# Masked graph attention on one core: pairs of query tiles, groups of 1024 keys, an unrolled program

## The chip, the cores and the metric

One NeuronCore of a Trainium2 chip runs the whole kernel. The metric is device time in microseconds (us) of one launch, the median of the timed runs. TensorE multiplies, ACT (ScalarE) evaluates functions, DVE (VectorE) does element-wise work and reductions, GpSimd (POOL) does simple element-wise work, and SyncE (SP) issues the transfers of the DMA engines, in its program's order.

## The reference, cut to what matters

N is 4096 nodes, D is 256 features. `h` is the rectified layer norm of `x`.

```
h   = relu(layernorm(x))
lQ  = masked_x @ Wlq ;  lK = h @ Wlk ;  lV = h @ Wlv + blv
s   = where(adj, lQ @ lK.T / 16, -1e9)                     # 4096 x 4096
gs  = (masked_x @ Wgq) @ (mean(h) @ Wgk).T / 16            # one global score a row
es  = masked_x @ Wes                                       # one own score a row
m   = max(rowmax(s), gs, es)
le, ge, ee = exp(s - m), exp(gs - m), exp(es - m)
den = rowsum(le) + ge + ee
res = le/den @ lV + ge/den * gV + ee/den * (masked_x @ Wev + bev)
out = x + maximum(res, masked_x)
```

## The kernel before

Matrices of the large products are split into a high and a low float16 half, and a product is made of three matmuls: low x high, high x low, high x high. `M = Wlq Wlk^T / 16` is folded first, so that the scores of a tile of 128 query rows are `q = mx M` (float32 matmuls, `project`, L523) times `h` transposed (`hT`). `q` is scaled by row and split on DVE (`q_split`, L732); the transposed halves `qT` come from a DMA transpose.

**Prologue.** Eight blocks g of 512 keys: DVE takes statistics of `x` (`h_stats`, L709) and scales (`h_scales`, L718), ACT applies them (`h_apply`, L432) and casts the high half, GpSimd subtracts for the low half (`h_low`), SP transposes (`transpose_h`, L244). TensorE already makes the scores of tile 0 and the value rows `V = h Wlv`, two V products of 256 keys a block (`v_product`, L592). Each engine has its own written order. A V product is made by TensorE at step g = 3 + b (`V_FIRST`), and moved out by ACT (`v_high`, L440) and DVE (`v_low`, L857) at step g = 5 + b (`V_SPLIT`); each pass of ACT or DVE over g does the layer norm of later blocks too.

**Main part.** One step per tile of 128 rows, 32 tiles, as a loop over pairs of steps. Inside a step there are eight blocks b of 512 keys. For each, TensorE makes the scores of the next tile (`scores`, L546, six matmuls of 512 columns into one of two banks) and the value products of four key chunks (`p_times_v`, L561), half a tile behind (`LAG = 4`). A chunk is a matmul of 512 columns (high half of p times both halves of V) and one of 256 (low half of p times high half of V), summed into `ps_u`. GpSimd turns `adj` into a bias of 0 or a large negative number, 1024 columns at a time (`mask_bias`, L379). DVE adds it to the scores while it moves them to `s32` and takes the block's maximum (`add_mask`, L771). When all eight are there `row_max` (L785) gives the negated row maximum, and ACT begins with the tile: `exp_block` (L452) and `p_high` (L458), 512 columns each; DVE subtracts for the low half (`p_low`, L802); SP transposes 1024 keys at a time (`transpose_p`, L260) into `pT`. `weights` and `combine` on DVE and `add_x` on GpSimd (L391) end a tile; `es_values` (L579) is a float32 product for the own term.

Of the kernel before, what the change touches and what calls it, by code (L numbers as in the profile page):

```python
# [5 lines left out]
P = 128  # L17
# [6 lines left out]
H_SCALE = 2.0 ** 11  # L24
P_SCALE = 2.0 ** 15
Q_TOP = 2.0 ** 14
# [3 lines left out]
W_SCALE = 2.0 ** 14  # L30
V_SCALE = 2.0 ** 10


class Tile:

    def __init__(self, pair, offset):
        self.t = pair * 2 + offset
        self.par = offset % 2  # L40
        self.half = pair + offset // 2


def due(n):

    return not isinstance(n, int) or n > 0


def build(nc, x, adj, mxT, mx, WlqT, WlkT, Wlv, blv, WgqT, WgkT, Wgv, bgv, Wes, Wev, bev, out):
    N, D = x.shape  # L50
    T = N // P
    NB = N // BLOCK
    DC = D // P
    SCALE = float(D) ** -0.5
    MB = 4
    MW = N // MB
    BPM = MW // BLOCK
    BPU = 2
    NU = NB // BPU
    LAG = 4  # L60
    EARLY = 5
    V_FIRST = 3
    V_SPLIT = 5
    HURRIED = 3

    XG = 4

    x_groups = x.rearrange("(g j p) d -> g p j d", p=P, j=CPB)

    with ExitStack() as ctx:  # L70
# [6 lines left out]
        def sem(name):  # L77
# [40 lines left out]
        wq_t = sb("wq_t", [P, DC, D])  # L118
        wk_t = sb("wk_t", [P, DC, D])
        wgq_t = sb("wgq_t", [P, DC, D])  # L120
        wgk_t = sb("wgk_t", [P, DC, D])
        wgv_sb = sb("wgv_sb", [P, DC, D])
        bgv_b = sb("bgv_b", [P, D])
        xbarT = sb("xbarT", [P, DC])
        xbar_bc = sb("xbar_bc", [P, DC, P])
        g_sb = sb("g_sb", [P, DC, D])
        w_sq = sb("w_sq", [P, DC, D])
        w_norm = sb("w_norm", [P, D])
        w_inv = sb("w_inv", [P, D])
        w_hl = sb("w_hl", [P, 2, DC, D], F16)  # L130


        adj8 = sb("adj8", [P, 2, N], U8)
        mxT_q = sb("mxT_q", [P, 2, DC, P])
        mxT_f = sb("mxT_f", [P, 2, DC, P])
        xm = sb("xm", [P, 2, 2, D])
        s32 = sb("s32", [P, 2, N])
        qT = sb("qT", [P, 2, 2 * DC, P], F16)
        q_hl = sb("q_hl", [P, 2, 2, D], F16)
        invc = sb("invc", [P, 2])  # L140
        invc_x = sb("invc_x", [P, 2])
        big = sb("big", [P, 2, 2])
        gs_es = sb("gs_es", [P, 2, 2])
        bmax = sb("bmax", [P, 2, NB])
        negm = sb("negm", [P, 2])
        psums = sb("psums", [P, 2, NB])
        mass = sb("mass", [P, 2, 3])
        rows_done = sb("rows_done", [P, 2, D])
        o_sb = sb("o_sb", [P, 2, D])


        bias = sb("bias", [P, N])
        rmax = sb("rmax", [P, 1])
        rclamp = sb("rclamp", [P, 1])
        rpow = sb("rpow", [P, 1])
        cinv = sb("cinv", [P, 1])
        cq = sb("cq", [P, 1])
        mloc = sb("mloc", [P, 1])
        m1 = sb("m1", [P, 1])
        den = sb("den", [P, 1])  # L160
        rden = sb("rden", [P, 1])
        r_u = sb("r_u", [P, 1])
        w3 = sb("w3", [P, 3])
        u1 = sb("u1", [P, D])
        un = sb("un", [P, D])
        e2 = sb("e2", [P, D])
        ur = sb("ur", [P, D])
        r1 = sb("r1", [P, D])
        r2 = sb("r2", [P, D])
        r3 = sb("r3", [P, D])  # L170

        p_hl = shared2[:, :].bitcast(F16).rearrange("p (u a k) -> p u a k", u=NU, a=2)
        pT = shared[:, :].bitcast(F16).rearrange(
            "p (u a c q) -> p u a c q", u=NU, a=2, q=P)

# [5 lines left out]
        s_wqk, s_wg, s_wgv, s_wlv, s_wev, s_bc = sem("s_wqk"), sem("s_wg"), sem("s_wgv"), sem("s_wlv"), sem("s_wev"), sem("s_bc")  # L181
        s_adj = [sem(f"s_adj{i}") for i in range(2)]
        s_mxq = [sem(f"s_mxq{i}") for i in range(2)]
        s_mxf = [sem(f"s_mxf{i}") for i in range(2)]
        s_xm = [sem(f"s_xm{i}") for i in range(2)]
        s_out = [sem(f"s_out{i}") for i in range(2)]

# [802 lines left out]
```

## Time and profile before

| | |
|---|---|
| median of 3 timed runs | 790.59 us (790.18 to 790.66) |
| span of the profiled execution, first to last instruction | 787.8 us |
| timed median less that span | 2.8 us |
| TensorE busy | 760.5 us, 97% |
| DVE busy | 613.9 us, 78% |
| ACT busy | 386.6 us, 49% |
| GpSimd busy | 222.5 us, 28% |
| mean granted TensorE clock | 0.996 of full speed |
| DMA engines' mean busy share, queue 1 | 74.5% |

The profile gives the span of the one profiled execution; it has no time of its own for the whole launch, so the timed median stands beside it. Busy is not the same as working at full rate: the end of each matmul is modelled, and adjacent ones overlap, so their rate is read from start to start.

### The profile page before, as it was taken

The page shows a single profiled execution, that of the slowest core. Times are in us where ns is not written, and L with a number is a line of the kernel's source. Part 1 is how long each engine was busy: PE and PEld are TensorE (multiplying, and loading weights), DVE is VectorE, ACT ScalarE, POOL GpSimd, SP SyncE. Part 2 cuts the span into 40 slices and gives each one's busy share as a digit, 9 for nine tenths or more (in the row PEclk, how much of TensorE's full clock was granted, in tenths as well). Part 3 has the DMA queues.
Part 4 walks back from the last instruction along what each step waited for, and adds up shares of the span by engine and source line. Part 5 has one row for each costly group of instructions (what it writes and reads, how often), then busy time and mean ns, then how long its engine had stood idle before and what let it go on. Part 6 is the DMA issues. An engine that isn't in the chain of part 4 may idle for free.

```text
span 787.8 us, 15535 instructions
## 1 busy us (share of the span) xinstructions
PE 760.5 (97%) x4200; PEld 424.8 (54%) x4200; DVE 613.9 (78%) x1811; ACT 386.6 (49%) x871; POOL 222.5 (28%) x175
## 2 busy tenths in 40 slices
PE   4799999999999999999999999999999999999995
PEld 3476555555555555555555555555555555555553
DVE  5967677788777778887777788877777888777775
ACT  5757553345555444455554434555544445555442
POOL 2642222332222323322223233223232332132200
PEclk9999999999999999999999999999999999999999
DMA  9983787967778778767677786766777876778656
GB/s 268 227 155 83 145 156 145 174 140 146 144 149 160 148 152 169 147 143 148 141 164 146 154 166 140 156 137 146 162 146 158 167 148 143 143 143 168 119 119 125
DMA packets 334786, 119.92 MB, mean 152 GB/s; under 512 B 303920, under 2 KB 330672, under 8 KB 334768
## 3 DMA queue, kind: packets, MB, share of 16 engines
q1 hardware_dynamic: 334768, 119.70, 74.5%
q8 instruction: 8, 0.13, 0.1%
q14 instruction: 10, 0.08, 0.0%
HBM read 39.98 MB, written 4.19 MB: 56 GB/s over the span
## 4 chain that ended last, share of the span: by engine, by line
PE 82%; issue 7%; DVE 5%; DMA 4%; SPq 1%; ACT 1%; POOL 0%; DVEq 0%; POOLq 0%
PE ps_scores L555 37%; PE ps_u L573 24%; PE ps_u L575 12%; PE ps_q L531 3%; PE ps_v L589 3%; DMA shared<-shared 3%; PE ps_v L602 3%; DMA shared<-x 1%; DVE st L713 1%; DVE shared L805 1%; DVE s L780 1%; DVE w_sq L888 0%; ACT shared L437 0%; DVE q_hl L752 0%; SPq L266 0%
## 5 line engine op out<-in xcount | busy, mean ns | idle before, releaser
L555 PE MATMUL ps_scores<-hT,qT 128*128 128x512 f16 x1536 | 374.3, 380 | 4.9 <-DVE bmax L780 3.5
L573 PE MATMUL ps_u<-v_rows,shared 128*128 128x512 f16 x1024 | 346.2, 379 | 5.8 <-DMA shared<-shared 5.8
L387 POOL TENSOR_SCALAR bias<-adj,big 128x1024 f32<-128x1024 uint8 x128 | 169.8, 1327 | 495.9 <-DVE bmax L780 270.4
L575 PE MATMUL ps_u<-v_rows,shared 128*128 128x256 f16 x1024 | 279.1, 273 | 0.0
L780 DVE CUSTOM_DVE_ANT_0 s<-ps_scores,bias 128x512 f32<-128x512 f32 x256 | 176.3, 689 | 98.4 <-PE ps_scores L555 82.6
L555 PEld LDWEIGHTS ps_scores<-hT,qT 128*128 128x128 f16 x1536 | 149.8, 98 | 160.2 <-issue 6.5
L805 DVE SCALAR_TENSOR_TENSOR shared<-s,shared 128x512 f16<-128x512 f32 x256 | 192.0, 760 | 20.1 <-ACT shared L464 20.1
L454 ACT ACTIVATE s<-s,negm,invc_x 128x512 f32<-128x512 f32 x256 | 204.5, 799 | 0.0
L506 ACT ACTIVATE mass<-gs_es,negm 128x2 f32<-128x2 f32 x32 | 9.5, 296 | 362.0 <-DVE negm L799 362.0
L573 PEld LDWEIGHTS ps_u<-v_rows,shared 128*128 128x128 f16 x1024 | 100.1, 98 | 131.4 <-DMA shared<-shared 9.7
L464 ACT ACTIVATE shared<-s 128x512 f16<-128x512 f32 x256 | 154.1, 614 | 0.0
L575 PEld LDWEIGHTS ps_u<-v_rows,shared 128*128 128x128 f16 x1024 | 100.2, 98 | 35.5
L396 POOL TENSOR_TENSOR o_sb<-rows_done,xm 128x256 f32<-128x256 f32 x32 | 36.0, 1126 | 42.5 <-DVE rows_done L855 42.5
L454 ACT ACTIVATION_READ_ACCUMULATOR s<-s,negm,invc_x 128x1 f32 x256 | 47.8, 187 | 0.0
L531 PE MATMUL ps_q<-mge,mxT_q 128*128 128x258 f32 (+1 forms) x128 | 34.3, 391 | 1.2 <-issue 1.2
L589 PE MATMUL ps_v<-wev_sb,mxT_f 128*128 128x256 f32 x128 | 32.9, 380 | 0.0
L531 PEld LDWEIGHTS ps_q<-mge,mxT_q 128*128 128x128 f32 x128 | 22.5, 195 | 7.3 <-issue 1.9
L589 PEld LDWEIGHTS ps_v<-wev_sb,mxT_f 128*128 128x128 f32 x128 | 21.8, 190 | 5.4
L376 POOL TENSOR_TENSOR v_rows<-shared,v_rows 128x1024 f16<-128x1024 f32 x8 | 17.2, 2149 | 24.1 <-ACT v_rows L450 24.1
L602 PE MATMUL ps_v<-w_hl,hT 128*128 128x256 f16 x192 | 22.7, 276 | 0.4 <-DVE v_rows L860 0.4
L602 PEld LDWEIGHTS ps_v<-w_hl,hT 128*128 128x128 f16 x192 | 18.9, 100 | 4.8 <-DVE v_rows L860 1.3
L780 DVE DVE_READ_ACCUMULATOR2_ANT bmax<- 128x1 f32 x256 | 21.3, 83 | 0.0
(75 smaller groups left out, 371.4 us busy)
## 6 DMA issues: line engine op xcount, KB each, us to landing
adj<-adj SPq DMA_DIRECT2D x32, 512.0 KB, 4.3
shared<-x SPq DMA_DIRECT2D x8, 512.0 KB, 6.1
mxT_q<-mxT SPq DMA_DIRECT2D x32, 128.0 KB, 2.6
mxT_f<-mxT SPq DMA_DIRECT2D x32, 128.0 KB, 2.2
xm<-x SPq DMA_DIRECT2D x32, 128.0 KB, 2.8
xm<-mx SPq DMA_DIRECT2D x32, 128.0 KB, 2.3
out<-o_sb SPq DMA_DIRECT2D x32, 128.0 KB, 2.3
shared<-shared SPq DMA_TRANSPOSE x128, 4.3
```

Of the source, the lines that this page charges most:

```text
L387: nc.gpsimd.tensor_scalar(bias[:, b * MW:(b + 1) * MW], adj8[:, k.par, b * MW:(b + 1) * MW], big[:, k.par, 0:1], big[:, k.par, 1:2], ALU.m ...
L396: nc.gpsimd.tensor_tensor(o_sb[:, k.par], rows_done[:, k.par], xm[:, k.par, 0], ALU.add).then_inc(s_o, 1)
L454: nc.scalar.activation(s32[:, k.par, b * BLOCK:(b + 1) * BLOCK], s32[:, k.par, b * BLOCK:(b + 1) * BLOCK], ACT.Exp, bias=negm[:, k.par:k.p ...
L464: nc.scalar.activation(p_hl[:, u, 0, at:at + BLOCK], s32[:, k.par, b * BLOCK:(b + 1) * BLOCK], ACT.Copy, scale=P_SCALE).then_inc(s_phi, 1)
L531: last = nc.tensor.matmul(ps_q[:, 0:cols], mxT_q[:, k.par, c], mge[:, c, 0:cols], start=c == 0, stop=c == DC - 1)
L555: last = nc.tensor.matmul(ps_scores[:, b % 2], qT[:, k.par, q_half * DC + c], hT[:, b * CPB:(b + 1) * CPB, h_half * DC + c, :], start=firs ...
L573: nc.tensor.matmul(ps_u[:, k.par], pT[:, u, 0, at + j], v_rows[:, kc, :], start=kc == 0, stop=False)
L575: last = nc.tensor.matmul(ps_u[:, k.par, 0:D], pT[:, u, 1, at + j], v_rows[:, kc, 0:D], start=False, stop=kc == NB * CPB - 1)
L589: last = nc.tensor.matmul(ps_e, mxT_f[:, k.par, c], wev_sb[:, c], start=c == 0, stop=c == DC - 1)
L602: last = nc.tensor.matmul(ps_v[:, n % 2, j * D:(j + 1) * D], hT[:, 2 * n + j, h_half * DC + c], w_hl[:, w_half, c], start=first, stop=h_ha ...
L780: nc.vector.tensor_tensor_reduce(out=s32[:, k.par, b * BLOCK:(b + 1) * BLOCK], in0=ps_scores[:, b % 2], in1=bias[:, b * BLOCK:(b + 1) * BL ...
L805: nc.vector.scalar_tensor_tensor(p_hl[:, u, 1, at:at + BLOCK], s32[:, k.par, b * BLOCK:(b + 1) * BLOCK], P_SCALE, p_hl[:, u, 0, at:at + BL ...
```

## The change

The kernel works on pairs of tiles and groups of 1024 keys: 16 pairs times 4 groups are 64 periods p, and one unit u is one tile of a period. The whole program is unrolled.

- **Scores.** Four blocks a period (`classic`): two tiles times two halves of 512 keys, each in its own bank (`ps_w`, `ps_x[1]`, `ps_v`, `ps_x[0]`). Each block is two `product` calls of three matmuls, one for each half of the 256 features, so eight products a period.
- **Values.** A chunk is three matmuls of 256 columns: high x high, high x low, low x high, into one 256-column sum for each tile. They run six periods behind the scores (`LAG_V = 6`), exponentials five (`LAG_E = 5`).
- **ACT.** `mask_bias` is now an ACT Identity with scale and bias by row, 1024 columns from uint8. Exponentials are 1024 wide and carry the factor of p in their bias, and `p_high` is a plain 1024-wide copy. ACT also scales and casts `q` (`q_scale`, `q_high`), in order among the exponentials.
- **DVE.** `out11`, `out12`, `out21`, `out22` take the place of `add_mask`; `p_low` is one 1024-wide subtraction; the scales of a pair's rows are found together (`q_rows`).
- **GpSimd** gets `q_low` and the bias terms of the row's end (`rest`, `add_rest`, `finish`).
- **Buffers.** `s32` holds five periods, `bias` three units, `p_hl` two, `pT` three; the row values of two tiles share a bank.
- **Prologue.** The scores of periods 0 to 3 (two tiles) are made there. `V_AT` gives the step at which V products are made and moved out, the same for TensorE, ACT and DVE.

The core of the diff:

```diff
+        V_AT = {3: (0,), 4: (1, 2), 5: (3, 4), 6: (5, 6), 7: (7, 8), 8: (9, 10, 11), 9: (12, 13, 14, 15)}
+            def transpose_p(u):
+                sp.wait_ge(s_plo, u + 1)
+                if u >= NPT:
+                    sp.wait_ge(s_pv, u - NPT + 1)
...
+            for p in range(4, NPER + LAG_V + 1):
+                if p + 1 < NPER and p >= 4:
+                    load_adj(p + 1)
+                if 0 <= p - LAG_E < NPER:
+                    transpose_p(2 * (p - LAG_E))
...
+                if 0 <= p - LAG_E < NPER:
+                    transpose_p(2 * (p - LAG_E) + 1)
...
+            def mask_bias(u):
+                p, t = u // 2, u % 2
...
+                if u >= NBI:
+                    v = u - NBI
+                    if v % 2 == 0:
+                        act.wait_ge(s_o11, v // 2 + 1)
+                        act.wait_ge(s_o12, v // 2 + 1)
...
+                nc.scalar.activation(bias[:, u % NBI].rearrange("p b k -> p (b k)"), adj8[:, p % 2, t], ACT.Identity,
+                                     bias=big[:, n % 2, 1, t:t + 1], scale=big[:, n % 2, 0, t:t + 1]
+                                     ).then_inc(s_bias, 1)
...
             for g in range(NB):
-                if HURRIED < g < NB - 1:
-                    h_deviation(g + 1)
                 h_apply(g)
-                if g <= HURRIED:
+                if g + 1 < NB:
                     h_deviation(g + 1)
                 h_high(g)
...
+                if g in (2, 4, 6):
+                    mask_bias(g - 2)
+                    mask_bias(g - 1)
+                for n in V_AT.get(g, ()):
                     v_high(n)
...
+            for p in range(4, NPER + LAG_V + 1):
+                if p < NPER:
+                    mask_bias(2 * p + 1)
+                u = 2 * (p - LAG_E)
+                live = 0 <= u < 2 * NPER
+                if live:
+                    if u % (2 * NG) == 0:
+                        act.wait_ge(s_negm, p // NG)
+                    exp_unit(u)
+                    if u % (2 * NG) == 0:
+                        side_exp((p - LAG_E) // NG)
+                    p_high(u)
+                n = (p + 3) // NG
+                if p % NG == 1 and 2 <= n < NP:
+                    q_scale(n)
+                if live:
+                    exp_unit(u + 1)
...
+                if p + 1 < NPER:
+                    mask_bias(2 * p + 2)
+                if live:
+                    p_high(u + 1)
...
+                if p >= 1:
+                    pe.wait_ge(free, p)
...
+                    nc.tensor.matmul(acc, pT[:, u % NPT, 0, j], v_rows[:, kc, 0:D], start=kc == 0 and t == 0,
+                                     stop=False, skip_group_check=True)
+                    nc.tensor.matmul(acc, pT[:, u % NPT, 0, j], v_rows[:, kc, D:2 * D], start=False, stop=False,
+                                     skip_group_check=True)
+                    done = nc.tensor.matmul(acc, pT[:, u % NPT, 1, j], v_rows[:, kc, 0:D], start=False, stop=end,
+                                            skip_group_check=True)
...
+                if b >= 1:
+                    for t in range(2):
+                        classic((b - 1) // 2, t, (b - 1) % 2)
+                for n in V_AT.get(b, ()):
+                    v_product(n)
...
                 if g >= 3:
-                    add_mask(Tile(0, 0), g - 3)
-                if g >= V_SPLIT:
-                    for n in v_steps(g - V_SPLIT):
-                        v_low(n)
-            for b in range(NB - V_SPLIT, EARLY):
-                for n in v_steps(b):
+                    p, b = (g - 3) // 2, (g - 3) % 2
+                    if b == 0:
+                        out11(p)
+                        out21(p)
+                    else:
+                        out12(p)
+                        out22(p)
+                for n in V_AT.get(g, ()):
                     v_low(n)
...
+                if low:
+                    p_low(u)
+                if p < NPER:
+                    out11(p)
+                m = (p + 3) // NG
+                if p % NG == 1 and 2 <= m < NP:
+                    q_rows(m)
+                if low:
+                    p_low(u + 1)
+                if p < NPER:
+                    out21(p)
...
+                if p < NPER:
+                    out12(p)
+                    out22(p)
```

## Rows read from the trace of the kernel before

**Rows 1.** The page: busy time of engines, share of the span, instructions.

```profile
PE 760.5 (97%) x4200; PEld 424.8 (54%) x4200; DVE 613.9 (78%) x1811; ACT 386.6 (49%) x871; POOL 222.5 (28%) x175
```

**Rows 2.** Timeline of TensorE in the middle: start us, us, engine, line, instruction.

```profile
403.64 1.04 PE L531 MATMUL ps_q<-mge,mxT_q 128*128 128x258 f32 x4
404.51 1.46 PE L555 MATMUL ps_scores<-hT,qT 128*128 128x512 f16 x6
405.81 0.38 PE L573 MATMUL ps_u<-v_rows,shared 128*128 128x512 f16 x1
...
407.11 1.46 PE L555 MATMUL ps_scores<-hT,qT 128*128 128x512 f16 x6
```

**Rows 3.** Groups by line: busy us, mean ns, idle us before, releasers.

```profile
L555 PE MATMUL ps_scores<-hT,qT 128*128 128x512 f16 x1536 | 374.3, 380 | 4.9 <-DVE bmax L780 3.5 <-DMA qT<-q_hl 1.5
L573 PE MATMUL ps_u<-v_rows,shared 128*128 128x512 f16 x1024 | 346.2, 379 | 5.8 <-DMA shared<-shared 5.8
...
L805 DVE SCALAR_TENSOR_TENSOR shared<-s,shared 128x512 f16<-128x512 f32 x256 | 192.0, 760 | 20.1 <-ACT shared L464 20.1
...
L387 POOL TENSOR_SCALAR bias<-adj,big 128x1024 f32<-128x1024 uint8 x128 | 169.8, 1327 | 495.9 <-DVE bmax L780 270.4 <-DVE big L756 225.5
```

**Rows 4.** Timeline of TensorE, prologue; idle time before in brackets.

```profile
23.23 1.46 PE L555 MATMUL ps_scores<-hT,qT 128*128 128x512 f16 x6 [1.48 <-DMA qT<-q_hl]
...
31.24 2.72 PE L555 MATMUL ps_scores<-hT,qT 128*128 128x512 f16 x6 [3.45 <-DVE bmax L780]
...
37.33 1.47 PE L555 MATMUL ps_scores<-hT,qT 128*128 128x512 f16 x6
38.66 2.79 PE L602 MATMUL ps_v<-w_hl,hT 128*128 128x256 f16 x24
41.29 0.54 PE L618 MATMUL ps_u<-ones,v_rows 128*128 128x1 f16 x16
```

**Rows 5.** Timelines of TensorE and GpSimd, the end of the span.

```profile
770.46 0.38 PE L573 MATMUL ps_u<-v_rows,shared 128*128 128x512 f16 x1 [3.35 <-DMA shared<-shared]
...
782.00 0.27 PE L575 MATMUL ps_u<-v_rows,shared 128*128 128x256 f16 x1
...
784.76 0.72 POOL L396 TENSOR_TENSOR o_sb<-rows_done,xm 128x256 f32<-128x256 f32 x1 [8.57 <-DVE rows_done L855]
```

**Rows 6.** Timeline of ACT in the middle.

```profile
402.68 0.80 ACT L454 ACTIVATE s<-s,negm,invc_x 128x512 f32<-128x512 f32 x1
...
403.47 0.61 ACT L464 ACTIVATE shared<-s 128x512 f16<-128x512 f32 x1
```

**Rows 7.** Timeline of ACT, prologue.

```profile
30.15 2.06 ACT L437 ACTIVATE shared<-shared,nb_h,rs_h 128x256 f32<-128x256 f32 x4
32.24 1.06 ACT L450 ACTIVATE v_rows<-shared 128x1024 f16<-128x1024 f32 x1
33.22 0.30 ACT L428 ACTIVATE sd<-mv,eps_sb 128x4 f32<-128x4 f32 x1
```

**Rows 8.** Timeline of DVE, prologue.

```profile
15.86 0.42 DVE L736 TENSOR_REDUCE rmax<-ps_q 128x1 f32<-128x256 f32 x1
...
17.07 0.48 DVE L752 TENSOR_SCALAR q_hl<-ps_q,cq 128x256 f16<-128x256 f32 x1
...
31.01 0.17 DVE L722 RECIPROCAL rs<-sd 128x4 f32<-128x4 f32 x1
...
33.10 0.69 DVE L780 CUSTOM_DVE_ANT_0 s<-ps_scores,bias 128x512 f32<-128x512 f32 x1
```

**Rows 9.** The transposes of line 266, from issue to landing.

```profile
DMA to landing us min/median/max: 4.2/4.3/7.1
```

**Rows 10.** Windows of the prologue: busy us by engine, granted clock.

```profile
core 0: us, PE busy (x) PEld busy (x) DVE busy (x) ACT busy (x) POOL busy (x), PEclk, DMA share, GB/s
...
31.30:34.60 3.30, 3.30 (x10) 1.37 (x11) 3.23 (x14) 3.27 (x7) 1.22 (x1) 0.50 1.12 262
34.80:38.00 3.20, 3.20 (x41) 2.59 (x39) 3.17 (x13) 3.17 (x7) 3.20 (x3) 1.00 1.01 192
```

More of the change, by code:

```diff
@@ L130, in build @@
[L130 to L144, printed above, removed]
@@ L161, in build @@
[L161 to L174, printed above, removed]
+        rmax = sb("rmax", [P, 2])
@@ L209, in build @@
+        s_ru, s_f, s_top = sem("s_ru"), sem("s_f"), sem("s_top")
         block = ctx.enter_context(nc.Block())
[L211 to L225 removed]
@@ new lines, in side_exp, with p_high @@
+            def side_exp(n):
+                for t in range(2):
+                    nc.scalar.activation(mass[:, n % 2, t, 1:3], gs_es[:, n % 4, t], ACT.Exp,
+                                         bias=negm[:, n % 2, t:t + 1]).then_inc(s_ge, 1)
+            def p_high(u):
+                p, t = u // 2, u % 2
+                act.wait_ge(s_exp, u + 1)
+                if u >= 2:
+                    act.wait_ge(s_pT[(u - 2) % NPT], ring(u - 2, NPT))
+                nc.scalar.activation(p_hl[:, u % 2, 0], s32[:, p % NS, t], ACT.Copy).then_inc(s_phi, 1)
@@ new lines, in side_scores, with q_form @@
+            def side_scores():
+                pe.wait_ge(s_gev, 3)
+                pe.wait_ge(s_wgv, 32)
+                for n, src in ((0, mxT_q), (1, mxT_f)):
+                    for t in range(2):
+                        for c in range(DC):
+                            last = nc.tensor.matmul(ps_side[:, n, t], src[:, t, c], mge[:, c, D:D + 2], start=c == 0,
+                                                    stop=c == DC - 1)
+                last.then_inc(s_side, 1)
+            def q_form(n, f, hl):
+                return qT[:, n % 2, hl * 4 + f]
@@ new lines, in es_values @@
+            def es_values(n):
+                pe.wait_ge(s_mxf, 16 * (n + 1))
+                if n == 0:
+                    pe.wait_ge(s_wev, 16)
+                if n + 3 < NP:
+                    pe.wait_ge(s_qf, 2 * (n + 4))
+                if n >= 1:
+                    pe.wait_ge(s_c2, 2 * n)
+                for t in range(2):
+                    for c in range(DC):
+                        last = nc.tensor.matmul(ps_q[:, t, 0:D], mxT_f[:, t, c], wev_sb[:, c], start=c == 0,
+                                                stop=c == DC - 1)
@@ L601, in v_product @@
                         for c in range(DC):
[L602 removed]
+                            last = nc.tensor.matmul(bank[:, j * D:(j + 1) * D], hT[:, 2 * n + j, h_half * DC + c],
                                                     w_hl[:, w_half, c], start=first,
@@ L701, in step_ @@
-            def step_(*a, project=True, **k):
-                step(*a, project_=project, **k)
-            schedule(pe, step_)
+            for t in range(2):
+                classic(3, t, 1)
+            for n in V_AT[NB]:
+                v_product(n)
+            side_scores()
+            pe.wait_ge(s_gev, 4)
+            for c in range(DC):
+                last = nc.tensor.matmul(ps_gv, xbar_bc[:, c], wgv_sb[:, c], start=c == 0, stop=c == DC - 1)
+            last.then_inc(s_gstep, 1)
+            for p in range(4, NPER + LAG_V + 1):
+                v = p - LAG_V
+                weigh = 0 <= v < NPER
+                n = (p + 3) // NG
+                if p % NG == 2 and 0 <= (p - 10) // NG < NP:
+                    es_values((p - 10) // NG)
+                if p % NG == 1 and 2 <= n < NP:
+                    project(n, D + 2)
+                at = 0
+                for b in range(2):
+                    for t in range(2):
+                        if p < NPER:
+                            classic(p, t, b)
+                        if weigh:
+                            p_times_v(v, at, at + 4)
+                            at += 4
+                for k in V_AT.get(NB + p - 3, ()):
+                    v_product(k)
```

1008 lines of the change are left out of this document (484 added, 524 removed).

## The prediction

> **What bounds the kernel now.** I read the page's engine row first, then the spacing of TensorE's instructions, then the first 80 us and the last 20, engine by engine. TensorE is busy 97% of the span [rows 1]. That figure hides nothing: in the middle, six 512-column products start 1.30 us before the next group (0.216 us each), four value chunks of a 512- and a 256-column product take another 1.30 us (0.325 a chunk), and the four float32 matmuls of one tile's projection 0.87 us, with no gap between [rows 2]. The `es_values` group has the same form; I price it alike. A tile then costs 8 x 1.30 + 8 x 1.30 + 2 x 0.87 = 22.5 us. All idle time ahead of value products is 5.8 us, and ahead of score products 4.9 us, over the whole span [rows 3]. So the steady part can't be shortened by better overlap. What there is to win or lose lies in the matmuls' own cost, in the start and in the end. From 31.24 us TensorE is dense [rows 4]; before that it starts its first score at 23.23 and idles 3.45 us. At the end it stalls 3.4 us at 770.46 and finishes at about 782.3; the last 5.5 us of the span are the row tail and the store [rows 5].
>
> **TensorE's work.** The score products stay 1536 of 512 columns: "eight" is four blocks of one period times two halves, each three matmuls, which is what there was. Per value chunk the columns stay 768, but as 3 x 256. A 24-matmul V product (all 256 columns, each with its own weights) takes 41.29 - 38.66 = 2.63 us, 0.1096 a matmul [rows 4], so a chunk costs 0.329 instead of 0.325: 1024 x 0.004 = +4 us. (From below nothing, from above 0.0096 x 1024 = +10 if the rounding of rows goes against me.) A period, four score blocks and 16 chunks, is 4 x 1.30 + 16 x 0.329 = 10.46 us; a pair of tiles 4 x 10.46 + 4 x 0.87 = 45.3.
>
> **The other engines in steady state.** An ACT exponential of 512 starts 0.79 us before the next instruction [rows 6]; a 1024-column copy takes 1.06 us, 0.95 of it before the next [rows 7]. For 1024 I take 1.28 (exp) and 0.95 (copy). The mask bias on ACT is not in the trace. Bounds: a 1024-column copy, 0.95, and four 256-column Relus with bias and scale from memory, 2.06 [rows 7]; I take 1.12, near the copy, since it is one instruction. ACT has six such per period: 6.7 us of 10.46. DVE: the mask add 0.61 and accumulator read, four times; the 1024-wide subtraction, from 0.76 at 512 [rows 3], between 1.0 and 1.5, I take 1.25. That is 5 us. GpSimd loses 128 mask instructions of 1.33 us [rows 3] and gets the row tail. What counts is the chain, since each engine runs in program order: ACT's mask bias for the second tile waits for `out12` of the period before; then mask, exp, copy, exp, mask, copy (6.7), then DVE's second `p_low` (1.25), `out21`, `out12` (1.3) and hops (0.2): 9.4 us per period. In one period in four `q_scale` waits on ACT for `cq`, behind the first `p_low`, `out11` and 1.5 us of row scales: with its own work +5.2 us. Four periods 4 x 9.4 + 5.2 = 42.8, under the 45.3 of TensorE. The queue on SP gives a second chain: `p_low`, issue of its transpose (about 2), the adj load behind it (4.3), mask 1.1, copy 1.0, `p_low` 1.25 = 9.7. Both fit, narrowly; each bank is free a whole period before TensorE wants it. I cost the steady part at TensorE's work.
> A section of the Trainium skill, ScalarE: Activation LUTs, "Rules for kernel authors", says multiplications and adds belong on VectorE, not ScalarE. By it, the move of the mask to ACT is the wrong way. The rows give ACT 3.8 us spare a period, so the sum has nothing for it; if it were wrong, it would be rival 1.
>
> **The prologue** is where the change loses. In the old one the copies of V product n run on ACT two key blocks after TensorE makes it, and TensorE cycles in 6.1 and then 4 to 5 us a block [rows 4]. In the new one product n, its `v_high` on ACT and its `v_low` on DVE all stand in the same step g (`V_AT`). Step g+1 on ACT (four Relus, then sqrt) waits behind `v_high`; DVE's `h_scales` waits for that sqrt, and the mask adds of key block g-2 come after it; TensorE's scores need these to free the bank; its V products come after the scores. That is a ring without slack.
> First scores: the first projection starts 13.28 as before, eight matmuls at 0.43 instead of four: 16.9. Reduction of 512 and scales: the old one takes 17.07 - 15.86 = 1.21 with a 256-wide reduction [rows 8], so 1.5: 18.6. ACT scales and copies (new) 1.4: 20.0; GpSimd subtraction of 512 1.1: 21.1; transpose 4.3 [rows 9]: 25.5. Two tiles' block 0: 28.2; block 1, 31.2; mean and second projection, 33.4. DVE's scales 1.5, then `w_hl` low and the first mask add: 36.7. Scores 2.6, V product 2.63, `v_high` 0.8: 42.8.
> The ring: Relus 2.1 [rows 7], sqrt 0.3, `h_scales` 0.5 and `h_stats` 1.6 (31.01 to 33.10) [rows 8], mask add 0.7, hops 0.4, two score blocks 2.6, two V products 5.25, `v_high` 0.6 = 14.0 us. Steps 4 and 5 pay it: 70.8. Step 6 has no `h_stats`: 12.4, 83.2. Step 7 has no scales: 9.9, 93.1. After the loop DVE has four mask adds and the mean, TensorE the g step, two score blocks and three V products before the next eviction: 15.8, 108.9. Side scores and the global value: 112.8. Period 4 with four V products: 5.2 + 10.5 = 128.5, eviction 1.5: 130. Second-pair projection and period 5's scores: 136.9. The first exponential waits on ACT for `v_high` of the last product, so the first value product can't start before 130.6 + 1.1 + 1.3 + 0.4 + 1.0 + 1.25 + 4.3 = 140; unit 1 waits for `q_scale`. I count 5.8 us for this filling: periods 6 and 7 end at 136.9 + 20.9 + 5.8 = 163.6.
> The clock: after the old kernel's 3.45 us of idleness the granted clock stood at 0.50 from 31.3 to 34.6 (1.2 GHz) and then 1.00 (2.4 GHz) [rows 10], and six products took 2.7 instead of 1.46 [rows 4]. That costs 1.7 us of work. The new prologue idles 3.4, 5.6, 5.8, 4.3 and 3.9 us (the steps less TensorE's part). I take four drops: +7, 170.6. Bounds: none, five. The Trainium skill, TensorE: Matmul & The Clock Gate, "HAM oscillation — how this bites in real kernels", describes this pattern of bursts and waits, each burst beginning at the low level; the one idle stretch of the trace agrees.
>
> **The rest.** From there: 56 periods of scores x 5.2 = 291; 62 periods of values x 5.26 = 326; 13 projections of a pair x 1.74 = 23; 16 x 1.74 = 28 for `es_values`: 668, which gives 838.6. Tail: the new lag is six periods, two after the last row maximum is known behind the old half tile. Eight units of pair 15 pass through two p_hl buffers: transpose 4.3 [rows 9], copy 1.05, subtraction 1.25, hops: 6.8 us for two units where TensorE needs 5.3. The first lands 13.5 after the last score, the last at 37.3; plus 2.6 and 1.7: 41.7 against 35.0 of work, +6.7. The last `es_values` stands behind the last value product, then two DVE adds 1.0, GpSimd add of 512 (0.72 at 256 [rows 5], so 1.2), max 0.7, GpSimd 1.2, store 2.6, hops: 7.3 instead of 5.5.
> Sum: 838.6 + 6.7 + 7.3 = 852.6 of span. The old span is 787.8 and its timed median 790.59: 2.8 lie around it. **Predicted 855 us**, 8% slower.
>
> **Rivals.** (1) The steady loop doesn't keep up. For it: chains of 9.4 and 9.7 us against 10.46, and transposes land in up to 7.1 us [rows 9]. If landing takes 1.5 us more and contention 0.4 on each subtraction, the chain passes TensorE's mean of 11.3 by 0.6: 56 x 0.6 = +34, 889 us. Against: TensorE waited for nothing in the old steady part. (2) The ring is looser: part of Relu, stats and V work overlaps, so that each step costs 9 instead of 14, no clock drop: 855 - 4 x 5 - 7 - 5 = 823. For it: the old prologue ran such steps in 4.4 to 6.1. Against: the program order as read. (3) Not slower: the ring doesn't exist because TensorE's queue always holds enough ready work, so that it is dense from its first score at 25.5. Remaining work then is 256 x 1.30 + 337 + 21 + 6 + 26 + 28 = 751; 776.5 + 6.7 + 7.3 = 790.5 of span, and 784 if the tail also doesn't stall: 787 to 793 timed. It decides only if the prologue's idle time after the first score is under about 2 us. I see no mechanism by which TensorE's own work shrinks: that the shared weights of two of three value matmuls load once gains nothing while loads lie under 256 columns [rows 4].
>
> **Numbers.** The unit for "same" is 0.2% (1.6 us), about what a measurement of this kernel can tell. The forecast 0.64 (its own range 838 to 872: no to five clock drops, filling 0 to 12, matmuls 0 to +10); rival 1 0.17; rival 2 0.11; rival 3 0.06, whose 787 to 793 lies astride the old time and is split evenly between faster and same; else 0.02, slower. Low 820 takes in rival 2, high 889 rival 1's centre; outside stay rival 3 and the far half of rival 1. Slower 0.94, same 0.03, faster 0.03.
>
> **What would show it.** Right: step 4's last V product is evicted near 57 us, first value product near 140 to 147, TensorE idle 3 to 6 us before the first score of steps 4 to 6, released by DVE's mask adds, which wait for the sqrt; the clock at 0.5 behind each; a pair of 45.3 us in the middle, without gaps. Wrong: idle time at `ps_x` or `ps_w` or before value products in every fourth period in the middle (rival 1); the first value product before 110 us (2), before 90 (3).

## The result and the profile after

The changed kernel takes **858.27 us** (median of 4 executions, 856.7 to 861.7), the kernel before 790.38 in the same session: ratio 1.087, 95% interval [1.0845, 1.0900]. Slower by 8.7%, 3.3 us above the forecast of 855. The profiled execution has a span of 854.9 us; before it was 787.8.

The page of the kernel after, engine row and granted clock in 40 slices of 21.4 us:

```profile
PE 784.0 (92%) x5232; PEld 535.0 (63%) x5232; DVE 451.0 (53%) x1155; ACT 506.4 (59%) x663; POOL 251.1 (29%) x223
...
PEclk9978799999999999999999999999999999999988
```

TensorE's share fell from 97% [rows 1] to 92%, and no other engine is near full: DVE went down from 78% to 53%. TensorE is still the bound in the long middle (9.9 us are lost there in 540); what the change adds lies in its waits before and after. I put TensorE's spacing at the full rate (0.216 us per 512-column product, 0.109 per 256-column one, 1.74 per pair's projection) against the time that it took, stretch by stretch of the trace. What is left is lost, idle or at half rate (an estimate, good to 3 us a row and to 1 us in the differences between the kernels):

| | before | after |
|---|---|---|
| TensorE's work at full rate | 746.8 | 749.4 |
| lost, first product to 25 us | 10.1 | 13.1 |
| lost 25 to 160 | 11.5 | 54.6 |
| lost 160 to 700 | 0.7 | 9.9 |
| lost 700 to TensorE's end | 4.7 | 14.7 |
| after TensorE's last product, and before its first | 14.0 | 13.3 |
| span | 787.8 | 854.9 |

Of the 67 us, 3 are lost before 25 us and 43 in the rest of the prologue, 9 in the long middle, 10 at the end; 2.6 are in the matmuls themselves.

TensorE's timeline of the kernel after, the scores of steps 4 to 7, the first value product, and the middle (start us, us, line, [idle us before <- releaser]):

```profile
46.46 0.58 PE L564 MATMUL ps_v<-hT,qT 128*128 128x512 f16 x1 [5.33 <-DVE bmax L793]
...
58.85 0.59 PE L564 MATMUL ps_w<-hT,qT 128*128 128x512 f16 x1 [5.34 <-DVE bmax L793]
...
70.35 0.58 PE L564 MATMUL ps_v<-hT,qT 128*128 128x512 f16 x1 [3.82 <-DVE bmax L793]
...
79.14 0.38 PE L564 MATMUL ps_w<-hT,qT 128*128 128x512 f16 x1 [1.73 <-DVE bmax L793]
...
132.93 0.28 PE L604 MATMUL ps_u<-v_rows,pT_base 128*128 128x256 f16 x1 [1.92 <-DMA pT_base<-p_base]
...
422.86 0.28 PE L604 MATMUL ps_u<-v_rows,pT_base 128*128 128x256 f16 x1 [0.86 <-DMA pT_base<-p_base]
```

Before, key blocks came every 4 to 6 us [rows 4]; now steps are 12.4, 11.5 and 8.8 us apart, and ahead of each step TensorE sits idle until DVE's mask adds free a bank (a step has two score blocks now and had one before). What DVE waited for is seen in one turn of the ring, all engines from 50.3 to 58.9 us:

```profile
50.35 1.47 PE L642 MATMUL ps_q<-r_base,hT 128*128 128x256 f16 x12
51.66 1.47 PE L642 MATMUL ps_u<-r_base,hT 128*128 128x256 f16 x12
...
53.17 0.60 ACT L400 ACTIVATE v_rows<-ps_u 128x512 f16<-128x512 f32 x1 [0.71 <-PE ps_u L642]
53.67 2.06 ACT L391 ACTIVATE p_base<-s,nb_h,rs_h 128x256 f32<-128x256 f32 x4
...
55.63 0.28 ACT L383 ACTIVATE sd<-mv,eps_sb 128x4 f32<-128x4 f32 x1
...
55.95 0.18 DVE L742 RECIPROCAL rs<-sd 128x4 f32<-128x4 f32 x1 [1.45 <-ACT sd L383]
...
56.45 1.40 DVE L734 BATCH_NORM_STATS2 st<-s 128x6 f32<-128x256 f32 x4
...
58.04 0.66 DVE L793 CUSTOM_DVE_ANT_0 s<-ps_w,bias 128x512 f32<-128x512 f32 x1
...
58.85 0.59 PE L564 MATMUL ps_w<-hT,qT 128*128 128x512 f16 x1 [5.34 <-DVE bmax L793]
```

Read it as one chain: TensorE's V product (L642), ACT's copy of it (L400), ACT's four normalisations and the sqrt behind that copy (L391, L383), DVE's scales and statistics, the mask add (L793), and only then TensorE's next scores, whose V products close the ring. In a turn TensorE has 5.2 us of work at full rate (twelve score products and two V products); step 4 took 12.39.

Windows of the same prologue, step 4, step 5, step 6, and step 7 to the first value product; the column after POOL is the granted clock:

```profile
46.46:58.85 12.39, 7.05 (x52) 4.29 (x53) 4.68 (x18) 6.00 (x10) 3.23 (x3) 0.78 0.32 64
58.85:70.35 11.50, 7.68 (x52) 4.48 (x53) 3.17 (x10) 4.76 (x9) 0.61 (x2) 0.80 0.82 120
70.35:79.14 8.79, 7.06 (x52) 4.29 (x53) 2.60 (x7) 4.47 (x8) 1.74 (x1) 0.85 0.46 98
79.14:132.90 53.76, 43.82 (x238) 26.86 (x238) 18.51 (x57) 19.91 (x28) 2.12 (x1) 0.84 0.17 40
```

A mean of 0.78 over 12.39 us with levels of 0.5 and 1.0 is 2 x 0.22 x 12.39 = 5.5 us at 1.2 GHz. The four rows give 5.5 + 4.6 + 2.6 + 17.2 = 30 us at the low level, against 3.4 in the whole old prologue [rows 10].

Groups by line of the kernel after (busy us, mean ns | idle us before, releasers), the answers to [rows 3]:

```profile
L604 PE MATMUL ps_u<-v_rows,pT_base 128*128 128x256 f16 x1024 | 281.1, 275 | 20.6 <-DMA pT_base<-p_base 20.5
L831 DVE TENSOR_TENSOR p_base<-s,p_base 128x1024 f16<-128x1024 f32 x128 | 164.8, 1288 | 223.3 <-ACT p_base L461 223.3
...
L434 ACT ACTIVATE bias<-adj,big 128x1024 f32<-128x1024 uint8 x128 | 158.2, 1238 | 189.8 <-DVE bmax L793 166.2 <-DMA adj<-adj 23.4
L447 ACT ACTIVATE s<-s,negm,invc 128x1024 f32<-128x1024 f32 x128 | 157.2, 1228 | 0.0
L461 ACT ACTIVATE p_base<-s 128x1024 f16<-128x1024 f32 x128 | 134.3, 1049 | 21.4 <-DMA pT_base<-p_base 19.7
```

The value products now wait 20.5 us in all for transposes (before 5.8). ACT's three big operations, among them the new mask bias at 1.24 us, fill 450 of its 506 us, and it still has 40% of the span free. In the tail DVE and ACT wait in turn (their timelines):

```profile
825.03 0.69 DVE L866 TENSOR_TENSOR t_sb<-t_sb,xm 128x512 f32<-128x512 f32 x1 [4.87 <-POOL t_sb L352]
...
831.36 1.06 ACT L461 ACTIVATE p_base<-s 128x1024 f16<-128x1024 f32 x1 [4.32 <-DMA pT_base<-p_base]
...
832.45 1.23 DVE L831 TENSOR_TENSOR p_base<-s,p_base 128x1024 f16<-128x1024 f32 x1 [3.38 <-ACT p_base L461]
```

DVE stands 4.87 us in the row work of the tile pair that is done, and a subtraction of the next unit stands behind it; ACT's copy waits for one of the two buffers until its transpose has landed.

### The profile page after: what moved, and what is told of

It is laid out like the page before. It is cut to its first block and busy times, and to the rows that moved or that the text cites. A ratio compares the mean times of both kernels' runs of the same rounds, so it can differ in the third digit from the quotient of the medians.

```text
span 854.9 us, 13952 instructions
## 1 busy us (share of the span) xinstructions
PE 784.0 (92%) x5232; PEld 535.0 (63%) x5232; DVE 451.0 (53%) x1155; ACT 506.4 (59%) x663; POOL 251.1 (29%) x223
## 5 line engine op out<-in xcount | busy, mean ns | idle before, releaser
L604 PE MATMUL ps_u<-v_rows,pT_base 128*128 128x256 f16 x1024 | 281.1, 275 | 20.6 <-DMA pT_base<-p_base 20.5
L831 DVE TENSOR_TENSOR p_base<-s,p_base 128x1024 f16<-128x1024 f32 x128 | 164.8, 1288 | 223.3 <-ACT p_base L461 223.3
L606 PE MATMUL ps_u<-v_rows,pT_base 128*128 128x256 f16 x1024 | 280.7, 274 | 0.0
L608 PE MATMUL ps_u<-v_rows,pT_base 128*128 128x256 f16 x1024 | 280.6, 274 | 0.0
L434 ACT ACTIVATE bias<-adj,big 128x1024 f32<-128x1024 uint8 x128 | 158.2, 1238 | 189.8 <-DVE bmax L793 166.2
L447 ACT ACTIVATE s<-s,negm,invc 128x1024 f32<-128x1024 f32 x128 | 157.2, 1228 | 0.0
L461 ACT ACTIVATE p_base<-s 128x1024 f16<-128x1024 f32 x128 | 134.3, 1049 | 21.4 <-DMA pT_base<-p_base 19.7
L604 PEld LDWEIGHTS ps_u<-v_rows,pT_base 128*128 128x128 f16 x1024 | 100.7, 98 | 65.2 <-DMA pT_base<-p_base 30.5
L606 PEld LDWEIGHTS ps_u<-v_rows,pT_base 128*128 128x128 f16 x1024 | 100.8, 98 | 34.8 <-issue 0.3
L608 PEld LDWEIGHTS ps_u<-v_rows,pT_base 128*128 128x128 f16 x1024 | 100.8, 98 | 12.3
L564 PE MATMUL ps_x<-hT,qT 128*128 128x512 f16 x256 | 99.0, 387 | 3.4 <-DVE bmax L793 3.4
L565 PE MATMUL ps_x<-hT,qT 128*128 128x512 f16 x256 | 98.8, 386 | 0.0
L566 PE MATMUL ps_x<-hT,qT 128*128 128x512 f16 x256 | 98.4, 384 | 0.0
L793 DVE CUSTOM_DVE_ANT_0 s<-ps_x,bias 128x512 f32<-128x512 f32 x128 | 88.2, 689 | 14.0 <-DVE p_base L831 10.2
L564 PE MATMUL ps_w<-hT,qT 128*128 128x512 f16 x128 | 49.7, 388 | 10.9 <-DVE bmax L793 10.9
L564 PE MATMUL ps_v<-hT,qT 128*128 128x512 f16 x128 | 49.9, 390 | 9.2 <-DVE bmax L793 9.2
L793 DVE CUSTOM_DVE_ANT_0 s<-ps_w,bias 128x512 f32<-128x512 f32 x64 | 44.2, 691 | 11.2 <-DVE p_base L831 10.2
L566 PE MATMUL ps_v<-hT,qT 128*128 128x512 f16 x128 | 50.0, 391 | 0.0
L565 PE MATMUL ps_v<-hT,qT 128*128 128x512 f16 x128 | 50.0, 391 | 0.0
L566 PE MATMUL ps_w<-hT,qT 128*128 128x512 f16 x128 | 49.8, 389 | 0.0
```

The lines of the kernel that those rows point to most:

```text
L434: nc.scalar.activation(bias[:, u % NBI].rearrange("p b k -> p (b k)"), adj8[:, p % 2, t], ACT.Identity, bias=big[:, n % 2, 1, t:t + 1], sc ...
L447: nc.scalar.activation(s32[:, p % NS, t], s32[:, p % NS, t], ACT.Exp, bias=negm[:, n % 2, t:t + 1], scale=invc[:, n % 4, t:t + 1], accum_o ...
L461: nc.scalar.activation(p_hl[:, u % 2, 0], s32[:, p % NS, t], ACT.Copy).then_inc(s_phi, 1)
L564: nc.tensor.matmul(bank, q_form(n, f, 1), keys(0), start=start, stop=False, skip_group_check=True)
L565: nc.tensor.matmul(bank, q_form(n, f, 0), keys(1), start=False, stop=False, skip_group_check=True)
L566: return nc.tensor.matmul(bank, q_form(n, f, 0), keys(0), start=False, stop=stop, skip_group_check=True)
```

## Experiments

In each, the kernel before ran on the same chip (789.5 to 789.7 us median). All are edits of the changed kernel except e5 and e6, which edit the kernel before; e11 and e12 add to e10, which joins four of the edits.

**e1: V products moved out one step later.** TensorE makes them where it did; ACT and DVE take most of them a step later, so that the sqrt and the mask adds don't stand behind them.

```diff
+V_OUT = {4: (0,), 5: (1, 2), 6: (3, 4), 7: (5, 6), 8: (7, 8, 9, 10, 11), 9: (12, 13, 14, 15)}
 (ACT's v_high and DVE's v_low:)
-for n in V_AT.get(g, ()):
+for n in V_OUT.get(g, ()):
...
-for n in V_AT[NB]:
+for n in V_OUT[NB]:
```

> The changed kernel, with each V product moved out (v_high on ACT, v_low on DVE) one step after TensorE makes it, instead of in the same step. Theory (ring in the prologue): steps 4 to 7 start their scores every 6 to 7 us instead of every 9 to 12.4, most of the half-rate stretches of the clock go too, the first value product moves from 132.9 to about 105 to 112 us, and the time falls from 858 to 830 (824 to 838). Rival (the steps are long for another reason, such as ACT's own work or landing transposes): another wait takes over, the steps keep 10 us or more, 850 or above.

Measured 832.15 us, ratio 1.053 [1.0500, 1.0568]: 26 of the 68 us, from the order of a few copies. Its V products of steps 4, 5 and 6 and the first score of step 7 (TensorE's timeline):

```profile
46.46 1.47 PE L644 MATMUL ps_q<-r_base,hT 128*128 128x256 f16 x12
...
52.07 1.47 PE L644 MATMUL ps_q<-r_base,hT 128*128 128x256 f16 x12
...
57.68 1.47 PE L644 MATMUL ps_q<-r_base,hT 128*128 128x256 f16 x12
...
63.85 0.39 PE L566 MATMUL ps_w<-hT,qT 128*128 128x512 f16 x1 [3.01 <-DMA hT<-v_rows]
```

Steps of 5.6 us instead of 12.4 and 11.5, with no idle time between; the first value product comes at 110.9 instead of 132.9. From 25 to 160 us the trace has 17 us at the low level where the kernel after has 34; that goes with the ring's idle stretches and is part of the gain. So for these 26 us the ring is the cause, and not the amount of work on any engine, which is the same. From step 6 on the steps are 8.8 and 8.6 us long again: ahead of step 7's scores TensorE waits 3.0 us for a transpose of `h`.

**e2: TensorE kept busy in the ring's idle stretches.** Added matmuls that nothing reads, ahead of the scores of steps 4 to 7.

```diff
+keep_busy({4: 70, 5: 70, 6: 50, 7: 20}.get(b, 0))   # 128-column matmuls into an unread part of ps_u
 if b >= 1:
     for t in range(2):
         classic((b - 1) // 2, t, (b - 1) % 2)
```

> The changed kernel with 70, 70, 50 and 20 added 128-column matmuls, whose sums are used by nothing, ahead of the scores of steps 4 to 7, where TensorE idles. The ring is left as it is; only the clock should change. Theory (half-rate stretches behind idle time cost 1.3 to 2.5 us in each step): the stretches of clock 0.5 between 45 and 83 us vanish, steps 4 to 7 shorten by 1.3 to 2.6 us each, time 851 (847 to 854). Rival (the clock lies under the waits): unchanged, 856 to 860. If the added matmuls end after the mask add, slower.

Measured 850.92, ratio 1.077 [1.0739, 1.0804]. With 11.7 us of work more it is 7.4 us faster. Its scores of steps 4 to 7:

```profile
48.29 0.38 PE L564 MATMUL ps_v<-hT,qT 128*128 128x512 f16 x1 [1.41 <-DVE bmax L800]
...
59.37 0.38 PE L564 MATMUL ps_w<-hT,qT 128*128 128x512 f16 x1 [1.40 <-DVE bmax L800]
...
68.94 0.38 PE L564 MATMUL ps_v<-hT,qT 128*128 128x512 f16 x1 [1.00 <-DVE bmax L800]
...
76.42 0.38 PE L564 MATMUL ps_w<-hT,qT 128*128 128x512 f16 x1 [0.59 <-DVE bmax L800]
```

A score product takes 0.38 us here where it took 0.58, and the steps 4, 5 and 6 are 11.1, 9.6 and 7.5 us instead of 12.4, 11.5 and 8.8. The ring is there without the low clock, which makes each turn 1.3 to 1.9 us longer; the first value product comes at 124.5 instead of 132.9.

**e5: the kernel before with value products as 3 x 256 columns.** Only the form of the value matmuls changes.

```diff
-nc.tensor.matmul(ps_u[:, k.par], pT[:, u, 0, at + j], v_rows[:, kc, :], start=kc == 0, stop=False)
+nc.tensor.matmul(ps_u[:, k.par, 0:D], pT[:, u, 0, at + j], v_rows[:, kc, 0:D], start=kc == 0, stop=False,
+                 skip_group_check=True)
+nc.tensor.matmul(ps_u[:, k.par, D:2 * D], pT[:, u, 0, at + j], v_rows[:, kc, D:2 * D], start=False, stop=False,
+                 skip_group_check=True)
```

> The kernel before with one part of the change: the 512-column value matmul split into two of 256, each with its own weight load. Theory: 2 to 4 ns for each of 1024 chunks, 792.5 to 794.5 (+0.3 to +0.5%). Rival 1: the split is free, 790. Rival 2: the weight loads of three short matmuls in a row do not fit under them, 20 ns or more a chunk, 810 or above.

Measured 790.97 against 789.54, ratio 1.0018 [1.0004, 1.0031]. The 256-column form costs 1.4 us (0.3 to 2.4 by the interval), less than I expected here and than the 4 us of the sum. That is 2% of the loss.

**e6: the ring made in the kernel before.** Its V products are moved out from step 3 on instead of step 5, that is, in the step in which TensorE makes them (a constant); TensorE makes them where it did.

```diff
-V_SPLIT = 5
+V_SPLIT = 3
```

> The kernel before with V_SPLIT = 3 instead of 5: V products are moved out in the step in which TensorE makes them, as in the changed kernel. Nothing else differs. Theory (ring): steps of 4.4 to 6.1 us become about 9 to 10 with idle TensorE ahead of the scores, released by the mask add, first value product 74.2 to about 90, time 790 to 808 (800 to 820). Rival (no ring; the steps of the changed kernel are long since each makes two score blocks and ACT has the mask): under 793.

Measured 811.49, ratio 1.029 [1.0257, 1.0330]; the first value product comes at 96.1, later than the 90 that I expected. Two of its score blocks (TensorE's timeline):

```profile
40.95 1.77 PE L555 MATMUL ps_scores<-hT,qT 128*128 128x512 f16 x6 [3.90 <-DVE bmax L780]
50.93 2.72 PE L555 MATMUL ps_scores<-hT,qT 128*128 128x512 f16 x6 [3.85 <-DVE bmax L780]
```

Steps of 10 us appear in a kernel that had 4 to 6, with the same releaser and again half-rate stretches behind them, and nothing else of the change is in it. Together with e1 this shows the ring by making it (22 us) and by undoing it (26 us).

**e7, e8, e9: the stalls behind the prologue, one each.** e7 gives p_hl a third buffer. e8 puts the row scales `q_rows` ahead of the first `p_low` in DVE's order. e9 puts DVE's `row_top` a period later, ahead of `p_low(u + 1)`, so that GpSimd has its part done.

```diff
 e7:
-p_base = sb("p_base", [P, 2 * GROUP])
+p_base = sb("p_base", [P, 3 * GROUP])
...
-if u >= 2: act.wait_ge(s_pT[(u - 2) % NPT], ring(u - 2, NPT))
+if u >= 3: act.wait_ge(s_pT[(u - 3) % NPT], ring(u - 3, NPT))
... (the buffer number is u % 3 for u % 2 wherever p_hl is written or read)
 e8 (DVE):
+if p % NG == 1 and 2 <= m < NP: q_rows(m)
 if low: p_low(u)
 if p < NPER: out11(p)
-if p % NG == 1 and 2 <= m < NP: q_rows(m)
 e9 (DVE):
+if p % NG == 3 and 0 <= (p - 11) // NG < NP - 1: row_top((p - 11) // NG)
 if low: p_low(u + 1)
 ...
-if p % NG == 2 and 0 <= (p - 10) // NG < NP: row_top((p - 10) // NG)
+if p == NPER + LAG_V: row_top(NP - 1)
```

> The changed kernel with three p_hl buffers instead of two: p_high of unit u waits for the transpose of unit u-3, no longer u-2. Theory (in the tail the two-buffer ring of transpose, copy, subtraction bounds the units): ACT's waits for landings (19.7 us) fall to a few, the tail after the last period's scores start shortens by 4 to 7 us, the middle changes by under 2: time 858 to 853 (850 to 855). Rival (transposes themselves or the stalls of VectorE set the tail's pace): under 2 us gained.

> The changed kernel with q_rows ahead of p_low and out11 in VectorE's order in the period in which q is made. Theory (TensorE's 10 us of stalls in the middle come from one late chain per pair, in which ACT waits up to 3.6 us for the scales, 53 us in all): ACT's wait for cq falls under 15 us, the lost time between 160 and 700 us from 9.9 to under 3, time 858 to 850 (847 to 853). Rival (the landing of transposes, not the late start, makes these stalls): cq's wait falls but the time stays within 3 us of 858.

> The changed kernel with row_top, VectorE's maximum that waits for GpSimd's sum, one period later (behind the first p_low and out11) except for the last pair. Theory (this wait holds up p_low by 4.9 us once in the tail, and by 1 to 3 us in the middle once per pair): VectorE's wait for GpSimd falls from 54 to under 15 us, the tail gains 3 to 5 us, the middle 0 to 5: 852 (848 to 856). Rival (hidden behind the transposes): under 2 us gained.

| | us | ratio, interval | what moved in the trace |
|---|---|---|---|
| after | 858.27 | 1.087 [1.0845, 1.0900] | |
| e7 | 853.81 | 1.081 [1.0789, 1.0839] | the tail 58.2 to 52.7 us; ACT's waits for transposes 19.7 to 11.9 |
| e8 | 846.58 | 1.072 [1.0699, 1.0735] | lost 160 to 700 us 9.9 to -0.2; lost 100 to 160 17.2 to 13.4; ACT's wait for `cq` 53 to 31, not under 15; the tail 58.2 to 60.5, with more of it at the low clock |
| e9 | 855.76 | 1.083 [1.0816, 1.0852] | DVE's wait for GpSimd 54 to 3.4 us; the tail 58.2 to 55.1; lost 160 to 700 9.9 to 7.6 |

The tail is counted here from the first score of the last period to the last value product. Windows of it, in the kernel after, e7 and e9:

```profile
787.79:846.01 58.22, 47.58 (x369) 37.52 (x367) 23.92 (x42) 26.93 (x38) 25.04 (x24) 0.94 0.77 145
791.22:843.91 52.69, 44.52 (x369) 36.08 (x367) 23.41 (x42) 26.10 (x36) 25.09 (x24) 1.00 0.79 160
791.68:846.79 55.11, 44.87 (x369) 35.91 (x367) 22.95 (x42) 27.26 (x38) 25.02 (x24) 1.00 0.79 155
```

The edit is not the only thing that differs: the kernel after has 2 x 0.06 x 58.2 = 7 us at the low level in its tail and the other two have none. At half rate that can be up to 3.5 us, which is more than all of e9's 3.1 and a part of e7's 5.5. So how much of either gain in the tail is the edit's own is open.

e8 takes away the whole loss of the middle. e9 takes away nearly all of a wait of 54 us and gains 2.5, less than expected: the wait went elsewhere. DVE's `p_low` (L831) waits 46 us longer for ACT's copy in e9 than in the kernel after (223.3 above):

```profile
L831 DVE TENSOR_TENSOR p_base<-s,p_base 128x1024 f16<-128x1024 f32 x128 | 169.5, 1325 | 269.0 <-ACT p_base L461 269.0
```

Most of the 54 us was idle time of an engine that was early. This is where a large number in the groups by line misled.

**e10: e1, e7, e8 and e9 together.**

> All of them with the later V move-out: three p_hl buffers, q_rows first, row_top later. Theory: the gains add up, since they lie in different stretches (prologue 26, middle 8, tail 8): 858 to 816 (810 to 822). Rival (they share one cause or a new bound takes over): 825 or above.

Measured 813.7 (810.0 to 815.2), ratio 1.029 [1.0262, 1.0321]. The four alone give 26.1 + 4.5 + 11.7 + 2.5 = 44.8, together 44.6: they add up. Lost now: 12.7 from 0 to 25 us, 29.7 from 25 to 160 us, -0.2 to 700, 8.4 to TensorE's end.

**e11 and e12: added matmuls in what is still idle.** e11 puts 45 ahead of step 3's scores and 40 ahead of step 7's; e12 has 143 more in the tail.

```diff
 e11:
+keep_busy({3: 45, 7: 40}.get(b, 0))
 e12, ahead of p_times_v(v, at, at + 4):
+if p == NPER: pe.wait_ge(s_o11, NPER)
+keep_busy({(59, 0): 18, (59, 8): 45, (61, 0): 25, (63, 0): 30, (63, 8): 25}.get((v, at), 0), ps_w[:, 0:P])
```

> e10_all with added matmuls of 128 columns (each about 0.056 us at full rate) into a part of ps_u that nothing reads, 45 ahead of the scores of step 3 and 40 ahead of those of step 7, where e10 idles 3.6 and 3.2 us on the path and its clock then stands at 0.5 for 35.9 to 42.7 and 63.2 to 70.0. The added work is 2.5 + 2.2 us and lies inside those idle stretches. Theory (idle stretches ahead of a burst cost twice, once as idle time and once as half rate): these two half-rate stretches of 6.8 us each are gone or shorter, the first value product comes 4 to 7 us before e10's 112.4, and the time is 806 to 811. Rival (the half rate stands beside waits for DVE, ACT and the transposes, which pass at the same moments anyway): first value product within 1.5 us of 112.4, the time 812 to 816. By either it stays above the kernel before, since the idle time and the later tail remain.

> e11_all_busy again, with 18, 45, 25, 30 and 25 more added matmuls of 128 columns (8.0 us of work in all at full rate) in the tail, ahead of the value products of periods 59 (both tiles), 61 and 63 (both tiles), where e10_all idles 1.0, 2.7, 1.5, 2.1 and 1.8 us. In e10 and e11 the tail is the same to 0.1 us until 19 us after the last period's first score, idle 2.6 us ahead of the same product; then e11's clock stands at 0.5 and e10's does not, and the last value product comes 51.7 us (e10) and 58.6 us (e11) after that score. Theory (the half rate alone makes e11's tail longer, by making row work and the last units late): with the idle stretches filled the clock stays at 1.00 until the last product, the tail is 50.5 to 52.5 us, and the time 807 to 811. Rival (the tails differ by where the transposes and the row work happen to fall, and the clock only goes along): the tail stays at 56 to 60 us and the time at 814 to 820, the added 8 us making it later still where they don't fit.

e11: 815.98, ratio 1.033 [1.0311, 1.0356]. Half of the expectation held: the first value product came at 108.4 instead of 112.4. But the time didn't fall: it lies in the rival's 812 to 816, whose other half, a first value product within 1.5 us of 112.4, doesn't hold. I had no case for that pair. The trace shows the 4 us given back in the tail. A value product of period 59, in e10 (first fence) and in e11 (second):

```profile
774.25 0.28 PE L606 MATMUL ps_u<-v_rows,pT_base 128*128 128x256 f16 x1 [2.39 <-DMA pT_base<-p_base]
```

```profile
770.93 0.28 PE L606 MATMUL ps_u<-v_rows,pT_base 128*128 128x256 f16 x1 [2.30 <-DMA pT_base<-p_base]
```

They stand 21.68 and 21.60 us after the first score of the last period (752.57 and 749.33), behind nearly the same idle time. The same window in each, e10 first; it begins just behind e11's product, and e10's starts at 774.25, inside it:

```profile
771.00:775.00 4.00, 1.61 (x15) 1.21 (x14) 1.24 (x7) 1.10 (x3) 2.47 (x3) 1.00 1.05 225
```

```profile
771.00:775.00 4.00, 4.00 (x22) 2.96 (x23) 0.00 (x0) 3.65 (x5) 3.64 (x6) 0.57 1.14 213
```

e10's clock stays at 1.00 (its next windows, to 789 us, too), e11's goes to 0.5. The tail, counted as above, is 59.0 us long in e11 and 52.0 in e10.

e12: 813.23, ratio 1.030 [1.0274, 1.0319], its profiled execution 812.7. The clock stays at 1.00 to the last value product, and the tail is 52.7 us long with 8 us of work more in it. The mechanism holds, since the rival's 56 to 60 didn't come, and all four executions of e12 (812.1 to 814.0) lie below those of e11 (815.2 to 819.4). The size of the time was off: 807 to 811 was expected, and e10's 813.7 is not measurably beaten. The medians of e10 and e12 lie closer together than the executions of either kernel, so the sizes of the clock's two gains (4 us in the prologue, 6 in the tail) are read from single traces.

## Why the prediction was right, and which terms were off

**The place and the mechanism held, and the closeness of the number is in good part luck** (below). The ring through `v_high`, the sqrt, `h_stats`, the mask add and the scores is the chain that the trace shows, with idle stretches of 5.33, 5.34 and 3.82 us before steps 4 to 6 (I said 3 to 6), released by DVE's mask adds. Before step 7 it is only 1.73 us. e1 and e6 confirm the ring from both sides. Rival 2, steps of 9 us and no clock drop (823), and rival 3, no ring (787 to 793), are out. The first scores came at 25.56 (said 25.5) and step 3's at 36.68 (said 36.7). Step 4's last V product was moved out at 53.8, not near 57, and the first value product came at 132.9, not at 140 to 147. The Trainium skill, TensorE: Matmul & The Clock Gate, "HAM oscillation — how this bites in real kernels", says that bursts apart from each other each start at the low level; the rows of steps 4 to 6 (0.58 us for a score product at their start, 0.38 in e2) agree. Step 7 doesn't start so: its first product takes 0.38 us, and the clock falls behind it.

**The ring was over-priced by 2.6 us a turn.** "A 24-matmul V product ... takes 2.63 us" reads the row of 24 matmuls [rows 4] as one product; it holds two. The trace after shows one as twelve matmuls, 51.66 - 50.35 = 1.31 us. A turn is then 14.0 - 2.6 = 11.4, and measured 12.4 with the clock low and 11.1 without (e2). All 16 products were charged on the path, so the prologue was 21 us too long. The sum of rival 3 has the right price, 21 us for all 16.

**The clock was under-priced.** I took four drops. At 1.2 GHz the prologue spends 30 us by the windows above, and 3.4 more at 137.9; at most half of that, 17 us, is lost, where I had 7. The filling also waits longer: between the starts of periods 4 and 8 TensorE idles 7.6 us (1.62, 0.67, 1.92 and 3.36, before 121.71, 129.55, 132.93 and 137.78), where I had 5.8. The errors offset each other: period 8 starts at 157.7 and not at 170.6, 13 us early.

**The steady part does stall, and the sign of rival 1 is there.** "I cost the steady part at TensorE's work" was wrong by 9.9 us from 160 to 700 us. A period without a projection or `es_values` is 10.42 us (said 10.46), but in most groups of four one period is longer, by up to 2 us, behind a wait ahead of a value product like that at 422.86 (0.86 us). I had the chain right (`q_scale` waits for `cq`, behind `p_low`) and its slack wrong: 42.8 against 45.3 a pair was a mean over four periods, and the stall sits in the one where it all falls together. e8 shows it. Rival 1's price (34 us) was far too high; its 0.6 us a period isn't what its terms give either, since 9.7 + 1.5 + 0.4 is 11.6, 0.3 above 11.3. ACT as the place of the mask costs nothing in the middle: e8 has it there too and loses nothing between 160 and 700 us. For the prologue no run separates it. An instruction takes 1.24 us; the 0.95 to 2.06 of the bounds held it, and my 1.12 was 10% low. (The 0.95 of the copy before its next instruction is 33.22 - 32.24 = 0.98 in [rows 7].) The advice of the Trainium skill in ScalarE: Activation LUTs, "Rules for kernel authors", against additions on that engine would have named the wrong cause: ACT's queue order cost 26 us (e1), its load is not shown to cost any.

**The tail was under-priced.** 6.7 us for eight units in two buffers; 14.7 are lost. The sum had no low clock there; the trace has 7 us of it, up to 3.5 us of loss, and e11 against e10 shows that a low clock in such a tail can move it by 7. With a third buffer and no low clock the tail is 5.5 us shorter (e7). `row_top`, whose wait for GpSimd stands before the last subtractions, was not in the sum; e9 puts the lost time from 700 us on slightly lower, at 13.5.

**TensorE's own work**: +4 said, +2.6 by spacing, +1.4 in e5.

Summed by place: period 8 at -12.9, the work behind it -2.5, the stalls +17.9 (24.6 instead of 6.7), the end -0.3. That is +2.2 on 852.6: the span of 854.9. So the forecast came within 3.3 us because a prologue 13 us too dear offset stalls 18 us too cheap: that is luck, and the ring alone is what the argument can claim.

**What stays open.** e10 is still 23 to 24 us above the kernel before. By its accounting 18 of them are lost between 25 and 160 us (29.7 against 11.5), where the first value product still comes at 112.4 and not at 74; that a pair of tiles has to be through its scores before the values may start would explain it, but no run here tests that. Nor does a run undo the other parts of the change (groups of 1024 keys, the unrolling) one by one.

## What to carry to other kernels

Where every engine runs its own queue in order, look for a ring: an eviction of this step, ahead of a preparation for the next one on the same queue, puts the whole chain into each step. In step 4 here no engine was over 60% busy (TensorE 7.05 of 12.39 us), and moving the evictions out one step later made steps of 12.4 and 11.5 us into 5.6. Move the eviction later before tuning any operation. A wait in the groups by line is worth only what its engine is late with: 54 us of DVE's waiting gave 2.5, and a reordering that touched a 53 us wait of ACT gave 12.

## What the runs showed of the hardware

- Idle time of equal length doesn't always set the clock. Behind 2.30 us the clock fell to 0.57 (mean of 4 us) in e11's tail, and behind 2.39 us, ahead of the same product, it stayed at 1.00 in e10. So one clock-sensitive stretch moved the tail by 7 us between two kernels that have the same tail, and a gain of 4 us early in the program was cancelled.
- Work that nothing reads can shorten a kernel: 11.7 us of added matmuls made it 7.4 us faster (e2), with the first score products of steps 4 to 6 at 0.38 us instead of 0.58.
- 256-column products with a weight load each start every 0.109 us; three of them in place of 512 + 256 columns cost 1.4 us in 1024 chunks (e5; 0.3 to 2.4 by the interval).
